# Scan stage: the product of step widths and input moves from VectorE (into PSUM) to GpSimd (into SBUF)

## What is computed

```python
u = einsum('bct,bcd->bdt', x, weights[conditions])
delta_r, B, C = split(einsum('bld,ed->ble', u, x_proj_w))    # 128, 16, 16
delta = softplus(einsum('blr,dr->bld', delta_r, dt_proj_w) + dt_proj_b)
A = -exp(A_log)                                              # 512 channels x 16 states
dA  = exp(delta[..., None] * A)
dBu = (delta * u)[..., None] * B[:, :, None, :]
h   = dA_t * h + dBu_t            # over the 64 tokens of a sequence, h = 0 at its start
y_t = sum over the 16 states of h * C_t
x   = x + y + u * D
```

## Time and profile before

| | us |
|---|---|
| median of 3 executions (lowest, highest) | 1910.63 (1907.96, 1910.76) |
| profiled execution, its own time | 1910.8 |
| its span, first to last instruction | 1909.2 |
| scan stage in it, first scan to last multiplication with C | 35.2 to 910.2 |

### The profile page before, as it was taken

One profiled execution on the slowest core, in us unless ns is written; L12 is line 12 of the kernel. 1 busy time (PEld: TensorE's weight loads), 2 busy tenths in 40 slices (PEclk: granted clock), 3 DMA queues, 4 the chain that ended last, 5 costly groups with the idle time before them and its releaser, 6 DMA issues.

```text
span 1909.2 us, 29992 instructions
## 1 busy us (share of the span) xinstructions
PE 1824.4 (96%) x9311; PEld 1268.8 (66%) x9311; DVE 1455.6 (76%) x2572; ACT 1262.9 (66%) x3938; POOL 1268.1 (66%) x1253
## 2 busy tenths in 40 slices
PE   6899999999999999988899899999999999999998
PEld 6777777777777777766355575756657575665764
DVE  7999999999999999999445765755656565565522
ACT  5878888888888888866355674655647465564621
POOL 4789999999999999988776654544545544450000
PEclk9999999999999999999899999999999999999999
DMA  5333323332333233322775534334343444431021
GB/s 206 130 129 146 136 95 135 146 135 101 130 146 146 105 115 146 133 78 72 232 209 164 151 100 121 109 108 131 94 132 100 116 118 110 120 93 60 30 66 40
DMA packets 117741, 230.67 MB, mean 121 GB/s; under 512 B 31364, under 2 KB 70292, under 8 KB 112464
## 3 DMA queue, kind: packets, MB, share of 16 engines
q1 hardware_dynamic: 84496, 163.48, 24.3%
q0 software_dynamic: 33088, 65.28, 12.8%
HBM read 212.09 MB, written 44.70 MB: 134 GB/s over the span
## 4 chain that ended last, share of the span: by engine, by line
PE 45%; ACT 3%; DVE 1%; issue 1%; DMA 1%; POOL 0%; DVEq 0%; ACTq 0%; SPq 0%; POOLq 0%
PE attn_psum L1946 12%; PE attn_psum L1962 12%; PE attn_psum L1876 4%; PE attn_psum L1863 4%; PE attn_psum L1856 4%; PE attn_psum L1903 3%; PE attn_psum L1847 2%; PE attn_psum L1980 2%; PE attn_psum L1888 1%; PE attn_psum L1837 1%; ACT xh L1587 1%; ACT th L1588 1%; ACT prob L1544 0%; DMA kv_at<-kv_scratch,new_now 0%; DVE prob L1698 0%
## 5 line engine op out<-in xcount | busy, mean ns | idle before, releaser
L1013 DVE TENSOR_TENSOR_SCAN hid<-scan_psum,dbu 128x1024 f32<-128x1024 f32 x256 | 592.0, 2313 | 0.0
L1185 PE MATMUL scan_psum<-hid,ident 128*128 128x256 f32 x2048 | 518.7, 383 | 29.7 <-POOL hid L506 29.5
L1185 PEld LDWEIGHTS scan_psum<-hid,ident 128*128 128x128 f32 x2048 | 377.3, 190 | 192.8 <-issue 106.4
L1698 DVE CUSTOM_DVE_ANT_0 prob<-attn_psum,mask 128x336 f32<-128x336 f32 x256 | 120.0, 505 | 273.1 <-PE attn_psum L1856 272.9
L506 POOL TENSOR_TENSOR hid<-hid,kv_at 128x1024 f32<-128x1024 f32 x128 | 306.2, 2405 | 27.6 <-DVE hid L1013 27.2
L506 POOL TENSOR_TENSOR hid<-hid,bc 128x1024 f32<-128x1024 f32 x128 | 306.1, 2404 | 23.0 <-DVE hid L1013 22.7
L1550 ACT COPY p_t<-attn_psum 112x384 f32<-112x384 f32 x256 | 122.4, 485 | 280.7 <-PE attn_psum L1863 280.7
L1962 PE MATMUL attn_psum<-w,ffn_hid 128*128 128x512 f32 x512 | 238.5, 595 | 4.9 <-DVE y_sb L1763 4.9
L1476 POOL DMA_INDIRECT kv_at<-kv_scratch,new_now x189 | 199.4, 1055 | 61.0 <-issue 57.0
L1946 PE MATMUL attn_psum<-xs_in,w 128*128 128x256 f32 x1024 | 232.4, 381 | 7.6 <-ACT xs_in L1556 6.6
L649 ACT ACTIVATE scan_psum<-kv_at,neg_a 128x252 f32<-128x252 f32 x512 | 211.6, 466 | 13.9 <-DVE hid L1013 12.3
(11 more groups left out here) (226 smaller groups left out, 3035.9 us busy)
## 6 DMA issues: line engine op xcount, KB each, us to landing
bc<-bc_scratch SPq DMA_DIRECT2D x16, 2048.0 KB, 7.5
kv_at<-bc_scratch SPq DMA_DIRECT2D x15, 2048.0 KB, 7.4
q_scratch<-qg SPq DMA_DIRECT2D x32, 260.0 KB, 2.0
early<-q_scratch SPq DMA_DIRECT2D x32, 260.0 KB, 3.8
x_pair<-in_x_pairs SPq DMA_DIRECT2D x32, 256.0 KB, 2.8
kv_scratch<-kvg SPq DMA_DIRECT2D x32, 256.0 KB, 2.1
a_scratch<-a_sb SPq DMA_DIRECT2D x32, 256.0 KB, 3.4
w_o<-x_scratch SPq DMA_DIRECT2D x32, 256.0 KB, 3.1
```

The costliest lines, as they stand in the source:

```text
L1013: nc.vector.tensor_tensor_scan(hid[:, k % RING, :, :].rearrange("p n t -> p (n t)"), decay[k % 2], dbu[:, k % RING, :, :].rearrange("p n t ...
L1185: mm = nc.tensor.matmul(yc, ident[:], hid[:, k % RING, i, :], start=False, stop=(k % 4 == 3 and i == 3))
```

## The change

`du` becomes an SBUF tile, and its product moves from DVE to POOL, behind POOL's sixth multiplication with C in a quarter (step 5); there it waits for the softplus addition, for ACT's copy of u and for DVE's 8 products with B. The space for it comes from `sq`, which shrinks from 12 to 4 rows (its values are never read; the sums beside them are), with waits of ACT on its own earlier squares. Waits that named `dve_du` name `pool_du`. The products with B are as before, but for where they read `du`.

```diff
@@ tiles
-        du = psum[:, 4, 0:2 * SUB].rearrange("p (c t) -> p c t", c=2)
+        du = sb("du", [P, 2, SUB])
...
-        sq = sb("sq", [P, G + H, HD])
+        sq = sb("sq", [P, 4, HD])
@@ gpsimd
+            def prepare(t, h, q):
+
+                pool.wait_ge(pool_dl, 4 * t + 2 * (q // 2) + 2)
+                pool.wait_ge(act_u, 4 * t + 2 * (q // 2) + 2)
+                wait(pool, dve_dbu, 8 * (4 * t + q))
+                at, c = SUB * (q // 2), 2 * (q % 2)
+                pool.tensor_tensor(du[:], delta[h][:, c:c + 2, at:at + SUB], u[h][:, c:c + 2, at:at + SUB], ALU.mult
+                                   ).then_inc(pool_du, 1)
...
+                    if k == 5 and parts.next_scan:
+                        prepare(*((t, h, q + 1) if q < 3 else (t + 1, 1 - h, 0)))
                     if k == 5 and parts.fourth:
...
             step(0)
             step(1)
+            prepare(0, 0, 0)
             quarters(pool, quarter)
@@ scalar
                     for i in heads:
-                        nc.scalar.activation(sq[:, G + i, :], qg[p][:, HD * i:HD * i + HD], ACT.Square,
+                        wait(act, act_ss, 12 * g + i - 3)
+                        nc.scalar.activation(sq[:, i % 4, :], qg[p][:, HD * i:HD * i + HD], ACT.Square,
@@ vector
                 if k == 0:
-                    dve.wait_ge(dve_du, 4 * t + q + 1)
+                    dve.wait_ge(pool_du, 4 * t + q + 1)
...
-            def prepare(t, h, q):
-
-                if q % 2 == 0:
-                    dve.wait_ge(pool_dl, 4 * t + q + 2)
-                wait(dve, dve_dbu, 8 * (4 * t + q))
-                at, c = SUB * (q // 2), 2 * (q % 2)
-                nc.vector.tensor_tensor(du, delta[h][:, c:c + 2, at:at + SUB], u[h][:, c:c + 2, at:at + SUB], ALU.mult
-                                        ).then_inc(dve_du, 1)
...
                 for k in range(8):
-                    if k == 7 and parts.next_scan:
-                        prepare(*after)
```

More of the change, by code:

```diff
@@ L232, in scan_block @@
         act_exp, act_y, act_kv, act_q = sem("act_exp"), sem("act_y"), sem("act_kv"), sem("act_q")
-        dve_du, dve_dbu, dve_h = sem("dve_du"), sem("dve_dbu"), sem("dve_h")
+        pool_du, dve_dbu, dve_h = sem("pool_du"), sem("dve_dbu"), sem("dve_h")
         act_z, pool_dl = sem("act_z"), sem("pool_dl")
@@ L481, in gather_first @@
                 if n == 0:
-                    pool.wait_ge(dve_du, 4 * (NT - 1))
+                    pool.wait_ge(pool_du, 4 * (NT - 1))
                     pool.wait_ge(act_exp, 32 * (NT - 1))
@@ L588, in take_u @@
                 act.wait_ge(pe_u, g + 1)
-                wait(act, dve_du, 2 * before)
+                wait(act, pool_du, 2 * before)
                 wait(act, pe_res, NCH * before)
@@ L690, in key_squares @@
                     for i in heads:
+                        wait(act, act_ss, 12 * g + H + i - 3)
                         nc.scalar.activation(sq[:, i, :], k_raw[:, i, :], ACT.Square,
@@ L1035, in _ @@
             place_tokens()
-            prepare(0, 0, 0)
             times_b(0, 0, 0, 0)
```

## The result

The changed kernel takes 2208.8 us (2208.4 to 2210.7) against 1910.7, a ratio of 1.157 (1.155 to 1.158): 298 us slower, where 254 were forecast, and 9 us above the range.

The account below looks back on a forecast made before the run. DVE was taken to bound the scan stage at 27.10 us a quarter. After the change POOL's queue plus held-up products would, adding 206 + 15 + 13 + 5 + 15 = 254 us to 1910.8: 2165 us, range 2135 to 2200.

Parts of the forecast that it names:

- What bounds the kernel: Scan stage: DVE sets the pace, busy for all 27.10 us of a quarter; POOL has 1.25 us left.
- the hold-up of each product: Products with B, now with two SBUF inputs, and POOL instructions reading SBUF block each other: 2165 us, chance 0.88.
- Part 1: Scan stage: `prepare` leaves DVE, 31 instructions at 0.58 us, -18.0 us if DVE still set the pace.
- Part 2: `prepare` on POOL costs 1.22 us, making POOL's work 27.47 us and POOL the bound, +0.37 us per full quarter.
- The rival that counts only this part: Products with B not held up, POOL's queue bounds: +5 us, 1916 us, chance 0.05.
- Part 3: Products with B reading `du` from SBUF cost POOL 1.09 us each, 8.7 a quarter; full quarter 35.7 us, sum 254 us.
- the ring of 4: Scan stage: how far DVE can be ahead of POOL while keeping up with POOL's pace.
- Part 4: `prepare`'s waits on POOL are hidden; up to 1.2 us a quarter if POOL lagged by two steps more.
- Part 5: ACT's squares wait for the square four before, about 1 us ago: costs nothing, with ACT 4.5 us idle per quarter.
- Out of step: Each product comes behind a started multiplication: step 5.6 us, 45 a quarter, up to 2470 us, chance 0.04.
- PE's clock falls: PE idles more and its clock drops: at half the clock 2730 us, chance 0.02.
- The signs: Expected in the trace: products averaging 2 to 3 us, most multiplications with C about 3.4, POOL busy nearly all quarter.

Follow-up runs that it names:

- the second experiment: The changed kernel with `du` copied by ScalarE from SBUF back to its old PSUM bank, where the products read it: 1913.5 us, ratio 1.0022.
- the first experiment: The kernel before with only the place of `du` changed: VectorE still makes it, but in SBUF; 2177.3 us, ratio 1.140.
- the seventh: The changed kernel plus a tiny GpSimd copy behind each weights fetch, on which GpSimd waits, so its queue empties for a moment: 2148.2 us, ratio 1.125.
- the bench: No kernel: one VectorE product beside GpSimd multiplications, computation left out, in some rows behind a DMA issue; four multiplications behind a DMA took 9.23 us.

## Why the prediction was wrong, point by point

**What bounds the kernel** was right: only the scan stage changed, and with it the time. So was the main mechanism, the hold-up of each product. What was wrong is one step of part 3 and the size of a hold-up.

**Part 1** held as far as it can be seen: DVE's work fell, and it was worth nothing, since DVE set no pace any more.

**Part 2** was right. `prepare` on POOL takes 1.23 us from start to start (622.45 - 621.22; 1.22 forecast). Without hold-ups POOL bounds at 27.38 us; its work of 27.47 was 0.1 us too high. The rival that counts only this part said 1916 us, and the second experiment measured 1913.5 for it.

**Part 3** has the failed step: "DVE keeps up with that: a step is product 1.12, scan 2.19 ... so DVE's next product waits 0.1 us and goes first again". The half about who goes first was taken from a single place, 114.72, and in the traces here it holds everywhere but behind a DMA issue of POOL, which is once in each quarter. I had counted the fetch as a help there ("the fetch of weights, in which POOL reads no tile", half a product hidden, -0.5 us). It was the opposite: it made the next product wait for two multiplications, its scan came late, and POOL stood idle for 3.37 us. Nor was DVE ahead by the ring of 4 there, but by one scan; whether a longer lead would spare POOL the idle time was not tested. The sum by its terms, for a full quarter: hold-ups 7 x 0.97 = 6.8 instead of 8.72 - 0.5 = 8.2, and the idle 3.37 instead of 0. That is 37.6 instead of 35.7, +1.9 for 23 quarters, 43.5 of the 46 us between the 254 forecast and the 299.8 between the two spans. The first four quarters took 5 us more than forecast, the last four 2.6 less.

The size of a hold-up was off as well, and the other way: 0.98 us, where the forecast had 1.09 from two halves (0.56 of the earlier trace rows and a difference of printed lengths of the earlier trace rows) and the range 1.02. With the measured size and no idle time the quarter is 27.47 + 8 x 0.97 = 35.2 us. The empty moment adds its 0.3 to that and showed 2148 us, inside the range of 2135 to 2200: without the idle time behind the fetch the forecast's range would have held.

That a product reads as fast from SBUF as from PSUM was right: unheld 1.19 to 1.20 us, from PSUM in the second experiment 1.20. The Trainium skill's "VectorE: DVE Perf Modes", in its section on the errata, has a PSUM source 62 cycles slower, an estimate of 65 ns. These don't show here either.

**Part 4.** `prepare`'s waits are hidden, nearly: DVE waits for `du` 15 times, 8.7 us in all, 4.2 of them ahead of the first product. **Part 5.** Nothing to be seen of the squares' waits.

**The rivals.** "Out of step" named the mechanism, a product behind a started multiplication, but as a general drift ("Three steps more"), with a chance of 0.04. Real was a fixed place once a quarter, and the range had no term for it. "PE's clock falls" came true in small, and not as the cause: the granted clock fell from 1.00 to 0.95 in the quarter, with PE busy for 29 of 37.6 us, and POOL's work, hold-ups and idle time make up the quarter. Late decays are there (DVE stands 4.79 us before the scan of 636.53, whose decays came behind ScalarE's wait for the keys, and 0.50 before the next, behind the sums). That they don't make POOL's idle time is seen in the first experiment (1.2 to 2.2 us of them a quarter, idle 3.37) and in the seventh (2.1 to 6.9, idle 0).

**The signs.** The products' mean of 2 to 3 us was 1.82, and most multiplications with C kept their 2.36 where 3.4 was forecast for most: in the quarter shown five of the seven hold-ups fell on POOL's other instructions, some of them only 0.2 us long by themselves. POOL was busy for 33.45 of 37.59 us and not for nearly all. The sign that the forecast named for being wrong, products that come behind a multiplication and wait out the next, came once in each quarter.

## What to carry to other kernels

Where VectorE and GpSimd share a loop, keep one input of each VectorE product in PSUM, or count 1 us (a little under the product's own length) for each on GpSimd's queue; here that was worth 268 us and the moved work 30. If both inputs must be in SBUF, look at the DMAs that GpSimd issues, and see that GpSimd waits for something soon behind each: a tiny copy of 0.3 us saved 2.1 us net a quarter. And a rule read from one place of a trace is a rule for that place: in the trace of before VectorE's one instruction with two SBUF inputs stood at a quarter's end, and in the quarter of the earlier trace rows POOL had waited once, for 0.33 us, between the fetch and it.

## What the runs showed of the hardware

- A VectorE product (128x1024 f32) that is held costs GpSimd 0.97 to 0.98 us where the product takes 1.21; it goes in at the end of the running instruction, in the middle of GpSimd's queue.
- Behind a DMA that GpSimd issues (indirect or plain) it does not: it waits until GpSimd's back-to-back run ends, up to 10.7 us in the bench, and GpSimd isn't lengthened (9.23 us for four). A wait in GpSimd's stream ends this (product 1.2 to 3.3 us); a COPY without a wait doesn't (8.10). What in the chip keeps it that way, no run shows.
- Inputs decide, not the output: with its output in PSUM and two SBUF inputs a product is held (3.13 us), with either input in PSUM it isn't (1.21). A GpSimd memset doesn't hold such a product (1.21), but it and a VectorE COPY do get in each other's way (memset 1.49 instead of 0.95 us).
